# A megakernel's order: the planner counts one table load for every change of ScalarE's tables, with offsets searched anew

## The reference

```python
x = L0_attn_x
xn = _layernorm(x, axis=-1)
x = x + _L0_attn_ref(xn, ...) + _L0_ffn_ref(xn, ...)   # Mamba scan; top-1 mixture of 8 experts
xn = _layernorm(x, axis=-1)
x = x + _L1_attn_ref(xn, ...) + _L1_ffn_ref(xn, ...)   # 16-head attention on arccos; two layers of local attention + GELU
return x
```

```python
g_dist = jnp.arccos(jnp.clip(cos, -1.0 + EPS, 1.0 - EPS)) * SPHERE_RADIUS
attn_score = (1.0 + g_dist / BANDWIDTH ** 0.5) ** (-D_INTRINSIC - ALPHA)
```

## Time and profile before

| | us |
|---|---|
| median of 3 runs | 2261.49 |
| lowest, highest | 2258.05, 2261.52 |
| the profiled execution, as timed | 2262.57 |
| its span, first to last instruction | 2261.3 |
| its mean granted TensorE clock | 0.863 |

### The profile page before, as it was taken

How to read it: one execution, slowest core, us unless ns; L and a number is a source line. 1 busy time by engine, 2 the same in 40 slices (tenths; PEclk the granted TensorE clock), 3 DMA queues, 4 the chain that set the end, 5 groups by cost and what they waited for, 6 DMA issues and landing times. The chain is left out here.

```text
span 2261.3 us, 40539 instructions
## 1 busy us (share of the span) xinstructions
PE 1788.6 (79%) x15282; PEld 1293.3 (57%) x15282; DVE 1697.8 (75%) x2517; ACT 1739.7 (77%) x2887; POOL 541.0 (24%) x270
## 2 busy tenths in 40 slices
PE   3668788998778977788688887886778786779787
PEld 2654566776466654555465565554556464556565
DVE  4878887775999698859976889749984799655552
ACT  2435786857888697887878988977589958887996
POOL 2231122222311222312232222302142121232230
PEclk9687778999889888898788887998988888889888
DMA  6751214350341133114310233013300242000000
GB/s 227 237 170 48 71 38 135 117 147 18 127 136 52 53 117 108 43 39 131 113 39 14 73 122 103 10 49 121 130 21 2 84 141 84 1 1 2 6 1 6
DMA packets 81651, 177.39 MB, mean 78 GB/s; under 512 B 10388, under 2 KB 41940, under 8 KB 81332
## 3 DMA queue, kind: packets, MB, share of 16 engines
q1 hardware_dynamic: 75632, 163.53, 22.4%
q0 software_dynamic: 2816, 7.21, 1.0%
q10 hardware_dynamic: 3012, 4.06, 0.5%
HBM read 161.92 MB, written 12.85 MB: 77 GB/s over the span
## 5 line engine op out<-in xcount | busy, mean ns | idle before, releaser
L1855 POOL TENSOR_TENSOR arena<-arena 128x1024 f32<-128x1024 f32 x128 | 316.3, 2493 | 622.8 <-ACT arena L1392 622.6
L1859 POOL TENSOR_TENSOR arena<-arena,rb 128x1024 f32<-128x1024 f32 x64 | 152.2, 2378 | 866.5 <-DVE rb L1711 866.5
L1579 DVE TENSOR_TENSOR_SCAN ps<-dA,ps 128x1024 f32<-128x1024 f32 x128 | 291.0, 2284 | 1.6 <-ACT dA L1351 1.0
L1153 PE MATMUL ps<-w_l_wqkv,arena 128*128 128x512 f32 x384 | 205.8, 670 | 23.0 <-DVE hB L1587 6.4
L844 ACT ACT_TABLE_LOAD x153 | 196.3, 1283 | 19.3 <-issue 16.6
L1413 ACT ACTIVATE arena<-arena 128x256 f32<-128x256 f32 x512 | 205.3, 402 | 2.0
L1351 ACT ACTIVATE dA<-mv,w_A_log 128x510 f32<-128x510 f32 x256 | 167.8, 711 | 42.2 <-DVE ps L1579 39.1
L1093 PE MATMUL ps<-gqT,gkT 8*128 8x256 f32 x1024 | 164.7, 460 | 38.9 <-DVE arena L1652 16.1
L1652 DVE TENSOR_SCALAR arena<-ps 128x1024 f32<-128x1024 f32 x128 | 155.0, 1217 | 51.3 <-PE ps L1093 50.7
L1573 DVE TENSOR_TENSOR ps<-BC,mv 128x1024 f32<-128x1024 f32 x128 | 181.6, 1425 | 12.9 <-ACT arena L1457 4.1
L849 PE MATMUL ps<-w_ident,arena 128*128 128x128 f32 x623 | 112.1, 326 | 99.5 <-DVE arena L1512 28.6
(11 more groups left out here) (223 smaller groups left out, 4507.7 us busy)
## 6 DMA issues: line engine op xcount, KB each, us to landing
BC<-bc_d SPq DMA_DIRECT2D x224, 512.0 KB, 4.2
BC<-in_experts SPq DMA_DIRECT2D x16, 514.0 KB
arena<-in_experts SPq DMA_DIRECT2D x15, 514.0 KB
mv<-in_experts SPq DMA_DIRECT2D x15, 514.0 KB, 3.4
arena<-in_x SPq DMA_DIRECT2D x8, 256.0 KB, 4.7
xnT_d<-arena SPq DMA_DIRECT2D x8, 256.0 KB, 3.0
hB<-xnT_d SPq DMA_DIRECT2D x8, 256.0 KB, 2.6
x<-in_x SPq DMA_DIRECT2D x8, 256.0 KB, 5.6
```

Of the source, the lines that this page charges most:

```text
L1153: e = t.matmul(lb(z), hT1[b][:, tt * P:(tt + 1) * P], w_lqkv[:, l, (w + z) * INNER:(w + z + 1) * INNER], start=True, stop=True)
L1579: v.tensor_tensor_scan(h_, flat2(dA[k % 2]), h_, 0.0, ALU.mult, ALU.add).then_inc(v_scan, 1)
L1855: g.tensor_tensor(la[m % 2][:, half], la[m % 2][:, half], cl[m % 2][:, half], ALU.subtract).then_inc(g_sub, 1)
```

## The change

The line L529 becomes `takes += LOAD_TIME`: the plan counts one load of 1.29 us for every change of tables, also for that from "ln" to "tan". `LATER` and `STREAM` get new values, 68 and 95 of them, found by a search with that count. Nothing else is touched: `STAGES`, `SWITCH`, `use()` and every emitting function are the same, and line numbers do not move. The diff, cut to the offsets that are spoken of:

```diff
@@ -90,32 +90,32 @@
 SWITCH = 127.0
 
-LATER = {"down": 17.13, "e_down": 0.92, "e_lg": -1373.3, "e_ln": 621.99, "e_load": -1698.97, "e_place": -129.783, "e_pre": 351.489,
...
-         "g_hd": -35.958, "g_ln": 938.103, "g_norm": -59.145, "g_oT": 238.89, "g_out": 718.35, "g_pow": 876.48, "g_qkv": 45.815,
-         "g_score": 49.652, "g_sq": 72.566, "g_sub": 570.978, "g_tan": 44.449, "gelu": -343.785, "heads": 43.677, "hid": -127.469,
...
-         "m_dt": 18.917, "m_du": 21.175, "m_ex": -16.259, "m_fin": 74.245, "m_hc": 137.244, "m_in": -23.847, "m_load": -295.604,
...
-         "norm": -15.561, "on": -140.182, "out": 284.565, "pt": -39.622, "pv": 82.873, "qkv": 47.209, "qn": -65.566, "rsum": -2.347,
...
+LATER = {"down": 18.164, "e_down": 0.391, "e_lg": -598.985, "e_ln": 78.027, "e_load": -534.944, "e_place": -272.346, "e_pre": 429.038,
...
+         "g_hd": -34.326, "g_ln": 1325.25, "g_norm": -78.469, "g_oT": 321.548, "g_out": 800.043, "g_pow": 567.055, "g_qkv": 44.797,
+         "g_score": 49.945, "g_sq": 74.09, "g_sub": 105.178, "g_tan": 50.448, "gelu": -298.892, "heads": 47.015, "hid": -332.474,
...
+         "m_dt": 78.843, "m_du": 30.796, "m_ex": -11.649, "m_fin": 78.045, "m_hc": 140.271, "m_in": -24.821, "m_load": 40.052,
...
+         "norm": -10.317, "on": -762.266, "out": 34.522, "pt": -35.544, "pv": 82.675, "qkv": 48.191, "qn": -433.43, "rsum": 0.494,
...
-          ("e", 42): -506.95, ("e", 43): 13.116, ("e", 44): 120.91, ("e", 45): -151.288, ("f", 0): -264.577, ("f", 1): 965.732,
...
-          ("l", 0): 9.585, ("l", 1): -1.65, ("l", 2): -21.803, ("l", 3): -10.56, ("l", 4): 3.21, ("l", 5): -95.803, ("l", 6): -154.583,
-          ("l", 7): -214.869, ("m", 0): -193.093, ("m", 1): 7.214, ("m", 2): 29.236, ("m", 3): 17.788, ("m", 4): -4.38, ("m", 5): 18.465,
-          ("m", 6): 31.906, ("m", 7): 313.502, ("o", 0): -664.133, ("o", 1): 53.635, ("o", 2): 157.041, ("o", 3): -16.87, ("o", 4): -90.478,
-          ("o", 5): -923.399, ("o", 6): 123.633, ("o", 7): 314.946, ("x", 0): -100.184, ("x", 1): -153.736, ("x", 2): -126.055,
...
+          ("e", 42): -365.493, ("e", 43): 20.697, ("e", 44): 198.934, ("e", 45): -325.744, ("f", 0): -1576.03, ("f", 1): 742.106,
...
+          ("l", 0): 2.917, ("l", 1): 0.458, ("l", 2): -20.535, ("l", 3): -8.827, ("l", 4): 3.997, ("l", 5): -93.658, ("l", 6): -150.622,
+          ("l", 7): -209.72, ("m", 0): -426.948, ("m", 1): 16.63, ("m", 2): 33.81, ("m", 3): 18.578, ("m", 4): -6.862, ("m", 5): 20.138,
+          ("m", 6): 33.051, ("m", 7): 244.539, ("o", 0): -521.258, ("o", 1): -704.991, ("o", 2): -1381.48, ("o", 3): 9.64, ("o", 4): -340.94,
+          ("o", 5): -170.922, ("o", 6): 254.54, ("o", 7): 38.929, ("x", 0): -151, ("x", 1): 1096.75, ("x", 2): 680.723, ("x", 3): -709.484,
...
@@ -526,7 +526,7 @@
                 takes = stages(unit)[stage][1]
                 if best[2] and best[2] != table:
-                    takes += LOAD_TIME * (2 if best[2] == "tan" and table == "ln" else 1)
+                    takes += LOAD_TIME
                     table = best[2]
```

More of the change, by code:

```diff
@@ L91 @@
 SWITCH = 127.0
-LATER = {"down": 17.13, "e_down": 0.92, "e_lg": -1373.3, "e_ln": 621.99, "e_load": -1698.97, "e_place": -129.783, "e_pre": 351.489,
-         "e_route": 144.702, "e_scat": 829.618, "e_store": -223.789, "e_tr": -184.595, "e_up": 44.242, "e_xn": -28.591, "e_xt": -830.714,
-         "f_ln": 818.98, "f_tr": -1660.36, "f_xn": -118.536, "f_yg": -111.816, "g_av": 89.144, "g_avT": -202.085, "g_ev": -784.392,
-         "g_hd": -35.958, "g_ln": 938.103, "g_norm": -59.145, "g_oT": 238.89, "g_out": 718.35, "g_pow": 876.48, "g_qkv": 45.815,
-         "g_score": 49.652, "g_sq": 72.566, "g_sub": 570.978, "g_tan": 44.449, "gelu": -343.785, "heads": 43.677, "hid": -127.469,
-         "l_weights": 625.975, "ln": -124.928, "ln2": 1.634, "lnT": -15.963, "m_B": -153.424, "m_C": 17.261, "m_bx": 50.752,
-         "m_dt": 18.917, "m_du": 21.175, "m_ex": -16.259, "m_fin": 74.245, "m_hc": 137.244, "m_in": -23.847, "m_load": -295.604,
-         "m_out": -935.123, "m_scan": 731.575, "m_sum": 14.942, "m_turn": -247.837, "m_weights": -173.243, "m_xp": 895.808,
-         "norm": -15.561, "on": -140.182, "out": 284.565, "pt": -39.622, "pv": 82.873, "qkv": 47.209, "qn": -65.566, "rsum": -2.347,
-         "score": -4.24, "shift": -70.641, "up": -71.786, "wo": 25.239, "x_load": 44.744}
@@ L104 @@
-STREAM = {("-", 0): 147.932, ("e", 0): -62.078, ("e", 1): 166.105, ("e", 2): -162.027, ("e", 3): 122.427, ("e", 4): 496.972, ("e", 5): -233.745,
[14 rows of a table removed]
+LATER = {"down": 18.164, "e_down": 0.391, "e_lg": -598.985, "e_ln": 78.027, "e_load": -534.944, "e_place": -272.346, "e_pre": 429.038,
+         "e_route": -189.368, "e_scat": -28.03, "e_store": -29.283, "e_tr": -112.377, "e_up": 30.954, "e_xn": -117.127, "e_xt": -919.116,
+         "f_ln": 943.891, "f_tr": -1158.8, "f_xn": 199.715, "f_yg": 353.385, "g_av": 86.985, "g_avT": -840.488, "g_ev": -364.647,
+         "g_hd": -34.326, "g_ln": 1325.25, "g_norm": -78.469, "g_oT": 321.548, "g_out": 800.043, "g_pow": 567.055, "g_qkv": 44.797,
+         "g_score": 49.945, "g_sq": 74.09, "g_sub": 105.178, "g_tan": 50.448, "gelu": -298.892, "heads": 47.015, "hid": -332.474,
+         "l_weights": 360.56, "ln": -224.396, "ln2": 2.013, "lnT": -13.544, "m_B": -53.141, "m_C": 523.724, "m_bx": 33.269,
+         "m_dt": 78.843, "m_du": 30.796, "m_ex": -11.649, "m_fin": 78.045, "m_hc": 140.271, "m_in": -24.821, "m_load": 40.052,
+         "m_out": -498.936, "m_scan": 992.769, "m_sum": 18.193, "m_turn": -219.064, "m_weights": -283.645, "m_xp": 1496.38,
+         "norm": -10.317, "on": -762.266, "out": 34.522, "pt": -35.544, "pv": 82.675, "qkv": 48.191, "qn": -433.43, "rsum": 0.494,
+         "score": -1.685, "shift": -59.11, "up": -58.564, "wo": 36.504, "x_load": -48.087}
@@ L120 @@
+STREAM = {("-", 0): 238.992, ("e", 0): -106.641, ("e", 1): 182.044, ("e", 2): -167.14, ("e", 3): 78.59, ("e", 4): 65.834, ("e", 5): -557.19,
[14 rows of a table added]
 LOADED = [15.0, 24.0]
```

## The result

The kernel after takes 2174.8 us in the median (2171.0 to 2180.6), before 2261.3 beside it: a ratio of 0.962, interval 0.960 to 0.965, 86 us less. The forecast of 2252 had the sign and a tenth of the size.

A forecast was written before the change was run, and what follows sets the result against it. No single engine bounds the kernel, but the order in which PE, ACT and DVE hand work on. Direct saving 0, plus 10 us, half of 21, from a better order: 2261.5 to 2252 us, range 2230 to 2279.

The forecast's parts named there:

- the sum: Whole kernel: direct saving 0; the re-search recovers between 0 and all of 21 us, half taken, 10 us.
- phantom: Second table load the old plan believed in at ACT's 35 ln-to-arctan changes, never run: 44.9 us in all.
- Part 1: ACT's ln-to-arctan changes: 35, each one load of 1.28 us with no drain behind it; direct saving 0 us.
- Part 2: Share of the phantom on the path: 9.0 us from 7 tail loads, 12.0 from the other 28, together 21 us.
- Part 3: New offsets: same pattern, different placement at its seams; table loads stay within 145 to 161, POOL and DMA cost nothing.
- rival (e): ACT's table changes: the count of two was right, so the new plan believes ACT early; 2275 us, chance 0.02.
- (d): Body: scan and attention overlap better, ACT rises from 80 to 81%, 17 us beyond the 10; 2235 us, chance 0.14.
- (a): ACT's waits on PE: phantom was a cushion for PE priced too low; 10 us slower, 2272 us, chance 0.15.
- (b): ACT's g_tan visits: cheaper changes invite 10 more visits, 10 us lost again; 2268 us, chance 0.09.

The follow-up runs named there:

- b_count1: The kernel before with only the planner's line changed to count one load per change, its old offsets kept: 2167.4 us, ratio 0.963.
- b_count105: The kernel before with a count of 1.05 loads in place of 2 per ln-to-arctan change, old offsets kept: 2236.1 us, ratio 0.988.
- a_load128: The kernel after with the planner's LOAD_TIME 1.28 in place of 1.29, nothing else: 2245.6 us, ratio 0.998.
- b_real2: The order of before, with a real second table load made at each of the 35 ln-to-arctan changes: 2287.4 us, ratio 1.010.
- a_clock087: The kernel after with the planner's CLOCK 0.87 in place of 0.88, which prices TensorE: 2268.3 us, ratio 1.008.

## Why the prediction was wrong

**The step that failed** is that of the sum which lets the search recover "between 0 and all of the 21 us". It ties the gain of a new order to the size of the mispricing, and took 10 us of it where 86 came. The runs showed that the one does not follow from the other: the line alone, with the old offsets, gave 83 us (b_count1), 2.3 us of phantom cost 2.5% (b_count105), 0.01 us in the price of a load 3.5% (a_load128), and the false price, searched, gave 0.972. The sign came right, but as far as the sum goes that was luck, since the size of the phantom had no part in it. What the count of two had done was to throw the planner out of an order that its offsets had been fitted to. The bound of the gain was not the phantom but idle time, 2261 - 1789 = 473 us of PE, the fullest engine, and 522 of ACT. I had both in the earlier trace rows without using them as a bound.

**The premise behind it** was that the old offsets were as well fitted to their count as the new ones to theirs. The text on record never weighed this. It could have been weighed in part: I noted that the inner offsets hardly move, and took it as a reason for a small gain. The same fact fits offsets that were already at the optimum of the count of one, with a wrong count put over them, and b_count1 and the plans above show that this is what they were. That they were in fact found by a search with the count of one, at 1.29 and 0.88, is inferred from that; no record of that search is here.

**Part 1**, the count: right. 35 changes, one load each, 1.29 us from load to next instruction; b_real2 has exactly 35 loads more. Behind 144 of the 153 loads of before, ACT's next instruction starts 1.29 or 1.30 us after the load did, and with a real second load ACT is busy 43 us longer (1782.8 against 1739.7) for 35 x 1.283 = 44.9. So rival (e) found nothing here. The Trainium skill, page "ScalarE: Activation LUTs", section "What ACT_TABLE_LOAD costs", adds a drain of about 1380 ns to a load of about 1283 ns; this trace agrees with the load and has no such drain.

**Part 2**, the share on the path: right in size, 21 us taken and 23 (15 to 30) measured. It priced something that was not the cause.

**Part 3**: "the same pattern with different placement at its seams" holds for the new offsets alone, which change 120 lines of ACT's list. It was wrong for the change, since the count by itself gives another order (990 of the 1028 lines). The loads stayed at 154, inside 145 to 161. Nothing shows a part of POOL or the DMAs: POOL's largest wait is now 700 us on ACT (L1855 on L1392), and DMA stands at 3 GB/s in the tail.

**The rivals.** (d), more than the phantom, came nearest, at 17 + 10 us where it was 86. Its sign in the profile, ACT's share of the body at 81% or more, came at 1431 / 1700 = 84%; but a_load128, with no gain, has 1397 / 1700 = 82%, so the sign proves little. Its price was a guess of one point of ACT's share, and its reason, more luck of the search, was not the cause: b_count1 needed no new search. (a), the phantom as a cushion: the waits of ACT on PE fell from 190 to 126 us; it did not happen. (b): one load more, not ten visits. Its price was also summed wrongly: 10 us lost again from the forecast's 2252 is 2262, not 2268. For the range: the two cases above 2.5% of gain had no row that I read as a bound, so it ended at 2230. Without knowing how the old offsets had been found, it had no ground to end there. How far down it should have reached the rows of before do not say: the idle time bounds the gain at 473 us and does not size it.

## What to carry to other kernels

Offsets that a search has found for a list scheduler, and every price in that scheduler, are one object: a change of about 1% in a price can lose the found order (3.5% of the time with the load, 4.5% with the clock here), though not every change does. So a price can only be judged by searching again on both sides with equal effort, and more than once. Before estimating what a reordered kernel gains, ask whether the old order was at an optimum of its own pricing; if that is unknown, the size of the mispricing is no bound; the idle time of the fullest engine is one, and a wide one. Where the planner can be run by itself, as here, a sweep of its prices answers the question before anything is built. And a kernel that gains from a truer cost model owes that gain to the truth only when a falser one, searched as long, doesn't give it too.

## What the runs showed that I had not expected

Two requests in a row for the same tables leave one load in the program (153, not 188). ScalarE's added table loads cost about half of their time in either order, 23 of 44.9 us (15 to 30) and 22 of 42.3 (some 10 to 35), although ACT is 77% busy in the one and 80% in the other. The granted clock of PE differs between orders of the same instructions (0.854 in a_clock087 to 0.879 in a_load128, 1801 to 1757 us of PE's busy time) without deciding the time: 0.879 came with a ratio of 0.998, 0.877 with 0.962.
